# Routing the last expert layer in two parts, inside the graph layers and the first expert blocks

## The reference, cut to what matters

```python
x = x + L0_gnn(ln(x))    # graph attention, 8 heads, then a 256-1024-256 feed-forward
x = x + L0_ffn(ln(x))    # 8 experts, 2 chosen per row, 256-256-256
x = x + L1_gnn(ln(x))    # two graph layers: h = (x + mean of neighbours) @ W.T + b; silu(layer_norm(h))
x = x + L1_ffn(ln(x))    # 8 experts, 2 chosen per row, 256-1024-256
```

```python
logits = xt @ Wr + br
top_p, top_idx = top_k(softmax(logits), 2);  weights = top_p / top_p.sum(-1)
xn = (xt - mean) * rsqrt(var + eps)                 # per row
h = gelu((xn * ln_g[e] + ln_b[e]) @ W1[e] + b1[e])  # 256 -> 1024, exact gelu
y = h @ W2[e] + b2[e]                               # 1024 -> 256
out = sum over the two chosen e of weights * y
```

## Time and profile before

| | |
|---|---|
| median of 3 runs | 2865.72 us (2862.45 to 2866.46) |
| the profiled execution | 2846.11 us |
| its span in the trace | 2844.2 us |
| mean granted TensorE clock | 0.882 of 2.4 GHz |
| TensorE (PE) busy | 2119.0 us, 75% |
| VectorE (DVE) busy | 1425.2 us, 50% |
| ScalarE (ACT) busy | 1231.4 us, 43% |
| GpSimd (POOL) busy | 792.9 us, 28% |
| DMA, mean over the span | 124 GB/s, 353.67 MB |

### The profile page before, as it was taken

How to read it: one execution, slowest core, us unless ns; L and a number is a source line. 1 busy time by engine, 2 the same in 40 slices (tenths; PEclk the granted TensorE clock), 3 DMA queues, 4 the chain that set the end, 5 groups by cost and what they waited for, 6 DMA issues and landing times. The chain is left out here.

```text
span 2844.2 us, 48302 instructions
## 1 busy us (share of the span) xinstructions
PE 2119.0 (75%) x10909; PEld 1686.5 (59%) x10910; DVE 1425.2 (50%) x3001; ACT 1231.4 (43%) x2549; POOL 792.9 (28%) x826
## 2 busy tenths in 40 slices
PE   8588865666766767677997067469999725999994
PEld 4344433554554545555886056369999724888884
DVE  8499984666666666676354322545443450111113
ACT  3399974555555555542323023134555411222221
POOL 4100005545555555522000532343031023001003
PEclk9799986989899998988996588789999757999997
DMA  4722215555555555521000345343534124555554
GB/s 152 296 75 76 77 64 136 151 139 151 153 150 149 148 146 142 144 80 39 0 0 1 139 122 149 106 112 96 146 100 124 49 73 146 194 199 207 194 204 146
DMA packets 184094, 353.67 MB, mean 124 GB/s; under 512 B 55506, under 2 KB 138903, under 8 KB 179287
## 3 DMA queue, kind: packets, MB, share of 16 engines
q1 hardware_dynamic: 130616, 199.44, 21.4%
q0 software_dynamic: 45520, 145.80, 18.4%
q10 hardware_dynamic: 7888, 7.60, 0.8%
HBM read 275.27 MB, written 77.47 MB: 124 GB/s over the span
## 5 line engine op out<-in xcount | busy, mean ns | idle before, releaser
L921 POOL DMA_INDIRECT kv_pair<-kv,gather_idx x448 | 430.8, 962 | 381.9 <-DVE R_kept L931 239.2
L1023 PE MATMUL p_edge_q<-QX_kept,onehot_turned 128*128 x904 | 292.6, 452 | 256.1 <-ACT onehot_turned L986 147.9
L1023 PEld LDWEIGHTS p_edge_q<-QX_kept,onehot_turned 128*128 128x128 f32 x904 | 177.8, 214 | 355.0 <-issue 328.5
L2179 ACT ACTIVATE experts_hidden<-experts_p_hidden,experts_pack 128x256 f32<-128x256 f32 x290 | 134.3, 472 | 465.4 <-PE experts_p_hidden L2220 392.5
L2220 PE MATMUL experts_p_hidden<-experts_turned,experts_pack 128*128 128x256 f32 x1160 | 278.4, 396 | 45.3 <-issue 20.7
L2657 PE MATMUL gnn_p<-gnn_y_high,gnn_counts_wide 128*128 128x256 f32 (+1 forms) x1250 | 307.9, 287 | 3.3 <-ACT gnn_counts_wide L2351 1.7
L2657 PE MATMUL gnn_p<-gnn_y_low,gnn_counts_wide 128*128 128x256 f32 (+1 forms) x1250 | 302.4, 283 | 0.0
L2220 PEld LDWEIGHTS experts_p_hidden<-experts_turned,experts_pack 128*128 128x128 f32 x1160 | 228.0, 198 | 86.5 <-issue 36.0
L2229 PE MATMUL experts_p_y<-experts_pack,experts_hidden 128*128 128x256 f32 x1160 | 268.1, 386 | 13.6 <-issue 13.3
L1031 PE MATMUL p_sums<-R_kept 128*128 128x265 f32 x896 | 265.5, 423 | 0.0
L2091 POOL DMA_INDIRECT experts_back<-slots_out,CSLOT x100 | 96.9, 969 | 546.8 <-issue 546.8
(11 more groups left out here) (445 smaller groups left out, 3448.7 us busy)
## 6 DMA issues: line engine op xcount, KB each, us to landing
experts_pack<-experts SPq DMA_DIRECT2D x29, 2052.0 KB
gnn_counts<-adj SPq DMA_DIRECT2D x400, 104.0 KB, 2.3
adj<-adj_counts SPq DMA_DIRECT2D x100, 208.0 KB, 1.9
experts_rows<-slots_in SPq DMA_DIRECT2D x60, 256.0 KB
experts_rest<-experts SPq DMA_DIRECT2D x59, 130.0 KB
slots_out<-experts_y ACTq DMA_DIRECT2D x29, 256.0 KB
slots_out<-experts_y SPq DMA_DIRECT2D x29, 256.0 KB
kv_pair<-kv,gather_idx POOLq DMA_INDIRECT x448
```

The costliest lines, as they stand in the source:

```text
L921: pool.indirect_dma_start(kv[r][:, j, :], None, a["kv"], bass.IndirectOffsetOnAxis(ap=idx[r][:, j:j + 1], axis=0)).then_inc(kv_in[r], 16)
L1023: mm = pe.matmul(pQ[q][:, j, 0:QW], oht[q][:, j, :], QX[:, at(w), :].squeeze(1), start=True, stop=True)
L2179: act.activation(hid[b][:, h, :], pH[h % NH][:, 0:BT], ACT.Gelu, bias=pack[b][:, B1 + h:B1 + h + 1]).then_inc(gelu_done, 1)
```

## The change

Four things:

1. `gnn_layers`, `moe_route`, `second_ln` and `experts` of the last layer become one block, `graph_and_experts`. The passes of both graph layers change order: first the 13 early destination tiles, then the 12 late ones. The last pass (25 source tiles, 12 destinations) so has the early 13 tiles to finish beside it, with their logits, their routing, their normed rows and their 26 scatters.
2. The slots are given in two parts. The early tiles fill blocks of 256 per expert; the late tiles fill what the early ones left open in an expert's last block and then new blocks. The first eight blocks in the order (`AHEAD = 8`) are full ones of early tiles alone; where there are fewer than eight, an empty block takes the place. The late tiles' finish, logits, routing, normed rows and 24 scatters go beside blocks 0 to 6. Blocks 0 to 8 are written out, the rest are a loop.
3. `moe(k, 0)`: the sum of `X` and the normed rows goes from POOL (after the scatter) to DVE (before it ends), and the counts are kept in a buffer of the stage.
4. `front` and `adjacency`: the edge keys are made on DVE in the loop over tiles of `front` (n = 16 to 19); their fills with -1 and 0 are POOL's; the constants are two arrays; the clearing of `ACC` and the table `WHERE` are done by POOL in `adjacency`.

The diff, cut to its core:

```diff
+AHEAD = 8
+NO = NB + AHEAD + 2
+UNIT_LO = (0, 4, 7, 10, 13, 16, 19, 22, NT)
 # front, SP and DVE
+            sp.dma_start(k["CF"][:], a["edge_consts"]).then_inc(edge_const_in, 16)
-            for n in range(16, NT):
+            begin(16)
+            lengths(10)
+            link(dve.tensor_copy(srcf[:], k["SRC"][:]))
...
 # adjacency, POOL
             pool.partition_all_reduce(mostall[:], k["MOST"][:], P, ALL_MAX).then_inc(all_ready, 1)
+            pool.memset(k["ACC"][:], 0.0)
+            pool.tensor_tensor(k["WHERE"][:], C[:, C_IOTA:C_IOTA + P].unsqueeze(1).to_broadcast(wide),
+                               C[:, C_WBASE:C_WBASE + NT + 1].unsqueeze(2).to_broadcast(wide), ALU.add)
 # moe(k, 0): POOL, then DVE
-            if not layer:
-                pool.tensor_tensor(normed[:], normed[:], X[:, 0:NT, :], ALU.add).then_inc(residual, 1)
+                dve.wait_ge(normed_ready, NT)
+                dve.tensor_tensor(X[:, 0:NT, :], X[:, 0:NT, :], normed[:], ALU.add).then_inc(residual, 1)
 # graph_and_experts, POOL: two scatters, then the gathers
+            for ph in range(2):
+                pool.wait_ge(slots_ready, 2 * ph + 1)
+                units = [u for u in range(UNITS) if SPAN[ph][0] <= UNIT_LO[u] < SPAN[ph][1]]
+                for u in units:
+                    for n in range(UNIT_LO[u], UNIT_LO[u + 1]):
+                        pool.wait_ge(normed_ready, n + 1)
+                        for j in range(TOPK):
+                            pool.indirect_dma_start(a["slots_in"], bass.IndirectOffsetOnAxis(
+                                ap=k["SLOT"][:, n, j:j + 1], axis=0), normed[:, n, :], None).then_inc(scattered[u], 16)
 # DVE beside the last pass and the first blocks
+            take(2, 0, EARLY)
+            spread_of(2, 0, EARLY)
...
+            choose(0)
+            second_factors(0)
+            place(0)
+            normalised(0, 3)
+            early_keys()
+            normalised(3, 8)
+            early_hits()
+            normalised(8, EARLY)
+            early_order()
+            gathered_slots(0)
+            copy_rows(0, 0, 0)
+            dve.wait_ge(wide_used, 4 * NT)
+            take(3, 0, 12)
...
+            for j in range(AHEAD + 1):
+                if j == 3:
+                    choose(1)
+                    second_factors(1)
+                if j == 4:
+                    normalised(EARLY, EARLY + 4)
+                    late_keys()
...
+                copy_rows(j + 1, (j + 1) % 2, (j + 1) // 2)
+                if j == 3:
+                    place(1)
...
+                finish(j, j % 2, j // 2)
 # PE: the last pass and the blocks
+            for m in range(NT):
+                for quarter in range(4):
+                    sum_up(3, m, (3 * NT + m) % 2, m == 0, m == NT - 1, range(3 * quarter, 3 * quarter + 3))
+                    if (m, quarter) in TIMES_AT:
+                        logits_times(TIMES_AT[m, quarter])
+                    if (m, quarter) in TURN_AT:      # m = 11, 12, 13
+                        logits_turn(TURN_AT[m, quarter])
+                if m == 17:
+                    count_members(0)
+                if m == 21:
+                    spread_keys(0)
+                if m == 23:
+                    sort_rows(0)
+            turn_rows(0, 0, 0)
+            for j in range(AHEAD + 1):
+                hidden(j, b, j // 2)
+                turn_rows(j + 1, 1 - b, (j + 1) // 2)
+                if j == 3:
+                    count_members(1)
+                if j == 4:
+                    spread_keys(1)
+                if j == 5:
+                    sort_rows(1)
+                for h in range(HC):
+                    if j == 2 and 1 <= h < 7:
+                        logits_times(PAIRED[0] + h - 1)
+                    if j == 2 and h < 6:
+                        logits_turn(PAIRED[0] + h)
+                    results(j, b, h)
 # ACT behind the last pass
+            deviation(3)
+            act.activation(warm[:], k["EPSC"][:], ACT.Gelu)
+            for j in range(AHEAD + 1):
+                step_of(j, j % 2, j // 2)            # 8 gelus
+                if j == 0:
+                    for p in range(4):
+                        silu(3, p)
```

More of the change, by code:

```diff
@@ L194 @@
 SOFTWARE = (["amax_kv_in"] + [f"kv_in{r}" for r in range(GTURN)] +
-            [f"scattered{layer}_{g}" for layer in range(2) for g in range(NGRP)] + [f"y_in{n}" for n in range(NT)])
+            [f"scattered{layer}_{g}" for layer, count in ((0, NGRP), (1, UNITS)) for g in range(count)] + [f"y_in{n}" for n in range(NT)])
 def at(i, n=1):
@@ L661, in adjacency @@
         pA = [s.enter_context(nc.psum_tensor(f"adj_p{b}", [P, 2, 4 * P], F32)) for b in range(2)]
-        count_in, step, summed = sem("count_in"), sem("step"), sem("summed")
-        countf, far = sb("count_wide", [P, QS]), [sb(f"src_distance{b}", [P, QS]) for b in range(2)]
-        placed, far_ready = sem("placed"), [sem(f"far_ready{b}") for b in range(2)]
+        step, summed, far_ready = sem("step"), sem("summed"), [sem(f"far_ready{b}") for b in range(2)]
+        far = [sb(f"src_distance{b}", [P, QS]) for b in range(2)]
         last_made = [sem(f"last_made{b}") for b in range(2)]
@@ L691, in _ @@
         def _(sp):
-            sp.dma_start(count[:], a["counting"]).then_inc(count_in, 16)
             for part in fills:
@@ new lines, in graph_and_experts @@
+    ident, ones, tri = (C[:, c:c + P] for c in (C_IDENT, C_ONES, C_TRI))
+    pid, index = C[:, C_WCOL:C_WCOL + 1], C[:, C_COUNT:C_COUNT + NO]
+    EARLY = HS // P
+    COUNT, FIRST = (EARLY, NT - EARLY), (0, EARLY)
+    SPAN = ((0, EARLY), (EARLY, NT))
+    PARTS = (((0, 4), (4, 7), (7, 10), (10, 13)), ((13, 16), (16, 19), (19, 22), (22, NT)))
+    TAKE = ((12,) + tuple(range(12)), tuple(range(2, 12)) + (0, 1), (12,) + tuple(range(12)), tuple(range(12)))
+    TAKEN = (0, EARLY, NT, NT + EARLY)
@@ new lines, in graph_and_experts @@
+    PAIRS = tuple(tuple(range(n, min(n + 2, hi))) for lo, hi in SPAN for n in range(lo, hi, 2))
+    PAIRED = ((EARLY + 1) // 2, len(PAIRS))
+    TURN_AT = {(11, 0): 0, (11, 1): 1, (11, 2): 2, (11, 3): 3, (12, 2): 4, (12, 3): 5, (13, 2): 6}
+    TIMES_AT = {(11, 1): 0, (11, 2): 1, (11, 3): 2, (12, 0): 3, (12, 3): 4, (13, 0): 5, (13, 3): 6}
+    COPY_AT = {12: (0, 1, 2, 3), 13: (4, 5), 14: (6,)}
+    RING, SUMS = 4, 8
+    HC, BR = FFN // P, BT // P
+    W1, W2 = 0, KD * FFN
+    B1 = W2 + HC * D
@@ new lines, in turn_rows, with hidden @@
+            def turn_rows(j, b, nxt):
+                pe.wait_ge(rows_in[b], 16 * (nxt + 1))
+                wait_if(pe, tT_ready, j)
+                for r in range(BR):
+                    for c in range(KD):
+                        mm = pe.transpose(pX[:, c, r * P:(r + 1) * P], rows[b][:, r, c * P:(c + 1) * P], ident)
+                mm.then_inc(t_done, 1)
+            def hidden(j, b, i):
+                pe.wait_ge(pack_in[b], 16 * (i + 1))
+                pe.wait_ge(tT_ready, j + 1)
+                for h in range(HC):
+                    c = h % NH
+                    if isinstance(j, int) and j == 0 and 0 < h < NH:
+                        pe.wait_ge(r_ready, TAKEN[3] + 2 * h)
+                    wait_if(pe, gelu_done, HC * j + h + 1 - (NH if h >= NH else 0) - (0 if h >= NH else h + 1))
+                    for d in range(KD):
+                        lo = W1 + d * FFN + h * P
+                        mm = pe.matmul(pH[c][:, 0:BT], pack[b][:, lo:lo + P], tT[b][:, d, :], start=(d == 0),
+                                       stop=(d == KD - 1))
+                    mm.then_inc(hidden_done, 1)
@@ new lines, in results @@
+            def results(j, b, h):
+                if h == 0:
+                    if isinstance(j, int) and j < 2:
+                        pe.wait_ge(r_ready, TAKEN[3] + 6 + 2 * j)
+                    wait_if(pe, out_ready, j - 1)
+                pe.wait_ge(gelu_done, HC * j + h + 1)
+                for r in range(BR):
+                    mm = pe.matmul(pO[b][:, r * D:(r + 1) * D], hid[b][:, h, r * P:(r + 1) * P],
+                                   pack[b][:, W2 + h * D:W2 + (h + 1) * D], start=(h == 0 and r == 0),
+                                   stop=(h == HC - 1 and r == BR - 1))
+                if h == HC - 1:
+                    mm.then_inc(e_done, 1)
@@ L2771, in chunks, with step_of @@
+            def step_of(j, b, i):
+                hidden(j, b, i)
+                turn_rows(j + 1, 1 - b, i + b)
+                for h in range(HC):
+                    results(j, b, h)
+            later_blocks(pe, step_of)
+SCRATCH = [("groups", (NG,), I32), ("adj", (NW, NQ, WD, QS), U16), ("kv", (NT * P, KVW), F32), ("slots_in", (NSLOT + 3 * BT, D), F32), ("slots_out", (NSLOT + 3 * BT, D), F32)]
 def chunks(w):
```

1456 lines of the change are left out of this document (948 added, 508 removed).

## The result

| | before | after |
|---|---|---|
| median, timed together | 2864.09 us (4 runs) | 2793.28 us (4 runs, 2781.45 to 2798.03) |
| ratio, 95% interval | | 0.9753, 0.9728 to 0.9778 |
| profiled execution's span | 2844.2 us | 2796.1 us |
| both again, on the chip of experiments 1 to 3 | 2846.10 us | 2779.68 us, ratio 0.9783 (0.9755 to 0.9810) |

The change is 70.8 us faster; 60 were forecast, 2806 for a measured 2793. The two spans alone show only 48 us. Most of the difference is a stage that the change doesn't touch: the attention over the edges took between 812 and 844 us in the 14 traces of this study.

The account below looks back on a forecast made before the run. It took PE's 105.3 us wait behind the last pass and block 0, slow beside POOL's scatters, as the bound. Terms -70 + 15 + 0 + 0 - 9 = -64, with overlap -60: 2786, plus 19.6 for the median: 2806 us (2790 to 2820; wider 2765 to 2850).

Parts of the forecast that it names:

- attention_max, -9: In attention_max, moving the clearing of ACC and WHERE to POOL beside the adjacency saves 9 us (6 to 9).
- Adjacency and front, 0: Keys end earlier, but ACT then waits longer for the same zero fills: 0 us (-6 to +2).
- The early part, -70 with bounds of -62 and -80: Early tiles' finish, routing and scatter beside the last pass: first hidden product at 2279 instead of 2348.6 us.
- source tile 13 is over at A = 2221: In the last pass, source tile 13 ends at 2221 us; the early scatter starts 20 us later.
- if every widening takes 10.85 us, H = A + 66: Last pass: with ACT's widenings as slow as a gelu, it ends with the scatter; first hidden product 66 us after A.
- The late part, +15 with bounds of -3 and +24: Late tiles' work beside the blocks costs 25 us, their scatter 24, against 34 that block 0 loses now.
- The first expert layer, 0 with up to 3: Removing POOL's 13.65 us sum gains 0, up to 3 us, as SP's 12 count loads set the end.
- DVE's new sum is hidden behind the scatter: In the first expert layer, the sum moved to DVE costs nothing beside POOL's scatter.
- The block count and the end, 0: Expert blocks of the last layer: no blocks added to 29, gathers and end unchanged, 0 us.
- (a): Rival: scatters cost nothing beside ACT's work, block 0's slowness being of the stage's start; 2768 us, chance 0.2.
- (b): Rival: more throttle and a lost cover of the turns, late scatter 30 us; 2830 us, chance 0.18.
- (c): Rival: late scatter holds ACT while open, pauses included, block 4's gelus taking 87 us instead of 14; 2869 us, chance 0.1.

Follow-up runs that it names:

- experiment 1: The kernel before and the changed kernel, both unedited, run again on one chip: 2846.10 us and 2779.68 us, ratio 0.9783.
- experiment 2: Changed kernel with the 26 scatters of the early tiles left out (output wrong): 2758.91 us, ratio 0.9700 to the kernel before.
- experiment 3: Changed kernel, last layer's scatters in a closed loop, a tile's two issued when the previous tile's have landed: 2769.80 us, ratio 0.9745 to the kernel before.
- experiment 5: Changed kernel with three small fills by POOL between the last layer's scatters, no wait for landings: 2767.78 us, ratio 0.9731 to the kernel before.
- Experiment 7: Changed kernel with the first expert layer's sum back on POOL after the scatter: 2779.18 us, ratio 0.9772 to the kernel before.
- experiment 11: Kernel before, without the change, both scatters in a closed loop and groups reported at once: 2788.68 us, ratio 0.9810 to the kernel before.

## Why the prediction came out right, step by step

**attention_max, -9: right.** 24.0 to 14.7 us.

**Adjacency and front, 0: right in size.** The adjacency is 1 us longer. The head start of 6 us hardly came about: ACT waits for POOL's maximum over the partitions until 101.98 us (101.69 before), and its first window begins 9.1 us into the stage instead of 10.1. The wait for the store behind the zero fills is shorter, not longer (10.7 us for 12.6), and ends 46.5 us into the stage instead of 46.0. So the fills set the time, as forecast.

**The early part, -70 with bounds of -62 and -80: mis-sized, it brought -47.** That is outside the bounds. The start of the scatter was right: some 20 us behind source tile 13 (2229.9 to 2249.7). Two terms of the sum were off. First, "source tile 13 is over at A = 2221": counted from the start of the graph layers it is over 11 us later than my sum had it. Half stands in the three passes ahead, 298 us instead of the 286 of before plus the 6 forecast; the rest in the start of the block (18.7 for 15.4 us) and the first 14 source tiles of the last pass (54 for 52). The turn's cover held: a source tile of a first pass takes 4.18 us, the forecast 4.2. Second, "if every widening takes 10.85 us, H = A + 66" was not the worst case: I had priced ACT alone. PE's products slowed to one per 1.4 or 2.1 us, ACT's idle time ahead of a widening reached 22.5 us, and the pass ended 10 us behind the scatter, at A + 62. Order and loads came behind that, as the sort stands in the pass, so H was A + 71. The bounds should have been widened for the engine that had no row of its own beside the scatter. Experiments 2, 3 and 5 show that without the slowing the pass is 87.0 us.

**The late part, +15 with bounds of -3 and +24: mis-sized, +1.** Block 0's stall of 12 us measured 11.4 to 11.8, against 36 us that block 0 lost before (34 in the sum); block 2's logits and roots 8.2 for 10.6, the keys 3.4 for 2.4. The late scatter was the wrong term: 24 us forecast, about 8 measured (22.4 to 14.8 us in block 5 when paced; block 4 keeps its 20 to 21). It has 24 DMAs with a pause of 4 us after 16, and the slowing begins only some 8 us into a run of them. So I take it that the pause made it cheap, as the pause in the first expert layer left SP's loads at 1.5 us for 6 us beyond its end; no run without the pause tests it. In size the row of the gathers (6 us) came nearer.

**The first expert layer, 0 with up to 3: wrong, -10.** "SP was held by its 12 count loads, so the end is SP's" was right; that the loads themselves depended on POOL's scatter was in the same rows, since they took 5.75 us each on average, and I didn't use it. The step that failed is "DVE's new sum is hidden behind the scatter": DVE's sum holds one of POOL's scatters for 5.6 us longer, and the loads take half as long. Experiment 7 shows it for the loads and the stage.

**The block count and the end, 0: right.** There are 29 blocks in both. Block 9 to the end takes 330.4 and 331.5 us after, 331.0 and 336.8 before.

So -47 and +1 stand for -70 and +15, and -10 for 0: errors of +23, -14 and -10 that nearly cancel. That the size came out was luck: three terms missed by 10 to 23 us each. The direction was not: the gap behind the last pass fell from 105 to 9 us for the reason given.

**The rivals.** (a), scatters that cost nothing: the trace disagrees, but its pass is what a paced scatter gives. (b) and (c) overrated the late scatter; the pause between tiles 20 and 21, which (c) feared, probably made it cheap. On the rule that I weighed, that DMAs issued from other engines than GpSimd are immune to the interference on the path by which GpSimd writes its rings (the Trainium skill, DMA: Bandwidth & Descriptors, SWDGE vs HWDGE vs iDMA): the interference meant there is DVE locking GpSimd out, and for that the trace agrees. While DVE's sum held POOL's scatter for 6.55 us, SP's loads went through at 1.5 us each. What the scatter does to the others is another effect: SP's 12 loads took 69 us beside it, 30 to 35 with the pause in it and 17 when it was paced, and PE, which issues no DMA, slowed as well. The word "immune" doesn't carry over to it.

## What to carry to other kernels

When one stage runs slow beside a burst of another engine's work, price that burst for every engine that will stand beside it after the change, not only for those whose rows show it now, and try a slower pace of the burst before moving the work: here a few lines that pace the scatter and report its groups at once brought 54 us to the kernel before, and the whole change 66. A lag in reporting (a unit counted as done when the next is issued) costs a unit's time, and grows when the pace is slowed: it was worth 12 us in the last layer and 18 in the first expert layer, where the slower pace alone showed no gain. And when a stall goes away, look again at what was built around it: DVE's sum gained 8 to 10 us beside the fast scatter and seems to cost as much beside the slow one. And where an untouched stage varies by 30 us between executions, compare stages, not spans.

## What was not expected of the hardware

GpSimd's indirect scatters of 128 rows of 1 KB, issued back to back at 1.27 us, slow the instruction issue of the other engines, from some 8 us after the first one until some 4 us behind the last: PE to one product per 1.4 or 2.1 us (0.12 otherwise), single ACT instructions by 8 to 22 us, SP's small loads from 1.5 us to as much as 11, and one DVE instruction by 7. At 2.1 to 2.6 us per scatter, or in pairs every 3.9 us, nothing is slowed: not the last pass (87.0 us), not block 5 (14.8), not SP's loads (1.5 us each), not blocks 1 to 5 of experiment 11 (14.3).

Gathers into the chip at 1.25 us do it, too. In the first expert layer of the kernel before, 8 of them, 10 us long, stretch a block from 4.05 to 12.1 us, with PE and ACT idle on "issue":

```profile
1703.50 1.00 POOL L2091 DMA_INDIRECT experts_back<-slots_out,CSLOT  x1 [45.21 <-issue]
...
1711.40 0.47 ACT L2179 ACTIVATE experts_hidden<-experts_p_hidden,experts_pack 128x256 f32<-128x256 f32 x1 [3.46 <-issue]
...
1711.92 2.08 PE L2229 MATMUL experts_p_y<-experts_pack,experts_hidden 128*128 128x256 f32 x4 [2.80 <-issue]
```

In the last layer 16 of them stretch two blocks by 4 to 10 us. DVE's sum of 128x6400 held one scatter of POOL for 5.6 us longer than its 0.96. What it is inside the chip that the scatters fill is not shown. It is not the DMA engines' time, of which 27% is used in the slowed stretch. The Trainium skill (Runtime: NRT & Kernel Launch, Instruction fetch mechanics) says that fetching instructions ahead is mostly hidden. The trace gives no sign against it: no packet of the instruction queues lies between 2250 and 2289, and the next one comes 1 to 2 us into source tile 24, as in all variants of the changed kernel, slowed or not. So a slow fetch is an unlikely cause of PE's slowness, though not excluded.
